# Cross-attention on one core: numerator and denominator from the same PV matmuls, in steps of two heads

## The chip, the core and the metric

The kernel runs on one core of a Trainium2 chip. The metric is the device time of one execution in microseconds (us); lower is better. The engines are PE (matrix multiply), ACT (activation functions), DVE (vector), POOL (GpSimd) and SP, which issues most DMA transfers. Each engine runs its own instructions in order and waits on semaphores for the others.

## The reference

One decoder layer over 64 sequences of 64 tokens, width 256, in float32: layer norm and causal self-attention, then cross-attention without weights, then a layer norm and a mixture of 8 experts (one per token) with a shared expert. The change is in the cross-attention. Its queries are the normalised rows, its keys and values the context rows, and each block is cut into 16 heads of 8 values:

```
qk  = einsum('bdm,bdn->bmn', qh, kh) * scale      # per head: 8 x 256 queries, 8 x 256 keys
sm  = softmax(qk, axis=-1)                        # over the 256 keys n
ret = einsum('bmn,bcn->bcm', sm, vh)              # per head: 8 values of c, 256 columns m
```

So in every head the two indices m and n run over the model's 256 columns, and the 8 values lie along the tokens. A tile is 128 tokens, which is 16 heads. There are NT = 32 tiles. After it, x2 = x1 + ret is normalised, multiplied with the router's weights, and each row is sent to its expert's place in DRAM (xg_d), scaled by the router's sigmoid.

## The kernel before, in words

The program has three stages one after the other: self-attention (`attention`), cross-attention with routing (`cross`), and the experts. This change touches only `cross`, which runs from about 1055 us to 1748 us of the span.

`cross` is a software pipeline over tiles. In the body for tile t, four tiles are in work: t itself (scores for the maximum), w = t-1, v = t-2 and z = t-3. Four bodies at the start and the last ones are written out; tiles 4 to 27 run in a hardware loop of U = 4 bodies, six times round (`tiles`, L849). Within a body every engine steps through 16 heads q, and the `if q == ...` lines of the `body` functions are the only thing that sets the order on each engine.

- `scores_x` (L1139, PE) makes queries by keys of one head in bankX (4 slots), `max_x` (L1052, DVE) reduces two heads at a time to minus the row maximum.
- `split_max` (L929, POOL) splits the 32 columns of maxima in a high and a low part (xhl). It is the first thing POOL does in a body; the last thing of the body before is `send`. `turn_max` (L1179, PE) transposes xhl, `evac_shift` (ACT) copies it, and SP writes it as two extra rows of the queries (L885).
- `turned_scores_x` (L1151, PE), eight heads behind, makes the scores transposed and already shifted in bankXT, which has 2 slots, one head each. It waits until the exponential of the head two before has been taken (`s_xe ... + q - 1`). `exp_x` (L1010, ACT) writes it to one of eight buffers xe.
- `results_x` (L1162, PE) multiplies four heads' exponentials with their values (cT: numerator) and again with a block of ones (onesx: denominator). Four heads use the four 32-column groups of the array at once. It runs four times per tile, at q = 1, 5, 9 and 13.
- `evac_sums` (ACT) copies both to nd, `invert` (DVE) takes the reciprocal of 128x256 denominators in four pieces, and `quotient`, `normalise` and `send` (POOL) divide, add x1, normalise, scale the row and send it with an indirect DMA. `stats_of`, `choose` and `place` (DVE) and `route` (PE) are the statistics and the routing in between.
- SP issues in each body, in this order: the shift rows, the context tile, the loads for tile t+1 (five transfers, 768 KB, L871 and L876), x1, and the stores of xn3 and x2.

Of the kernel before, what the change touches and what calls it, by code (L numbers as in the profile page):

```python
# [760 lines left out]
def cross(nc, A, G, NT, NRT):  # L761
# [6 lines left out]
    with ExitStack() as pb:  # L768
# [3 lines left out]
        def bank(name, n=1):  # L772
# [12 lines left out]
        ones = sb("onesx", [P, 4, 32])  # L785
        onesf = sb("onesf", [P, P])
        half_neg = sb("half_negb", [P, 1])
        spare_g, spare_v = sb("spare_gb", [P, 1]), sb("spare_vb", [P, 1])
# [4 lines left out]
        xe = [sb(f"xe{i}", [P, 2, D]) for i in range(8)]  # L793
        nd = [sb(f"nd{p}", [P, 2, D]) for p in range(2)]
        rden = sb("xrden", [P, D])
        num_ = sb("xnum", [P, D])
# [25 lines left out]
        s_xs, s_xm, s_hl, s_shp, s_shv, s_xst, s_xe, s_xp, s_nd, s_rd, s_num, s_x2 = (  # L822
            sem(n) for n in ("s_xs", "s_xm", "s_hl", "s_shp", "s_shv", "s_xst", "s_xe", "s_xp", "s_nd", "s_rd",
                             "s_num", "s_x2"))
        c_hl, c_ln, g_ln, s_var, s_rstd, s_norm = (
            sem(n) for n in ("c_hl", "c_lnb", "g_lnb", "s_varb", "s_rstdb", "s_normb"))
        s_f3p, s_f3, s_lg, s_top, s_esc, s_oh1, s_rank, s_pos, g_sc, c_fin = (
            sem(n) for n in ("s_f3p", "s_f3", "s_lg", "s_top", "s_esc", "s_oh1", "s_rank", "s_pos", "g_sc", "c_fin"))

        HEADS = [4 * j + (j + b) % 4 for b in range(4) for j in range(4)]  # L830
        LAG = 8
        QUARTER = D // 4
# [16 lines left out]
        def tiles(eng, body):  # L849

            def peeled(t):
                body((t // U, t % U), t < NT, 1 <= t < NT + 1, 2 <= t < NT + 2, 3 <= t)

            for t in range(FIRST):
                peeled(t)
            with eng.Fori(FIRST // U, LAST // U) as h:
                for p in range(U):
                    body((h, p), True, True, True, True)
            for t in range(LAST, NT + 3):
                peeled(t)  # L860
# [4 lines left out]
        def _(sp):  # L865
# [12 lines left out]
            def body(tile, one, two, three, four):  # L878
# [17 lines left out]
                if four:  # L896
                    z = prev(tile, 3)
                    zp = z[1] % 2
                    sp.wait_ge(s_norm, at(z) + 1)
                    sp.dma_start(G.xn3_d[bass.ds(at(z) * P, P), :], xn3[zp][:]).then_inc(s_fst[zp], 16)  # L900
                    sp.dma_start(G.x2_d[bass.ds(at(z) * P, P), :], x2[zp][:]).then_inc(s_fst[zp], 16)

            sp.dma_start(rw[:].rearrange("p k e -> p (k e)"), A["rw"]).then_inc(s_rw, 16)
            load((0, 0))
            sp.dma_start(G.wsh[:], A["wexp"][E]).then_inc(G.s_wsh, 16)
            tiles(sp, body)
# [5 lines left out]
        def _(pool):  # L912
            nc.gpsimd.memset(half_neg[:], -0.5)
            nc.gpsimd.memset(onesf[:], 1.0)
            nc.gpsimd.memset(ones[:], 0.0).then_inc(s_zc, 1)
            pool.wait_ge(s_zc, 1)
            for i in range(4):
                nc.gpsimd.memset(ones[:, i, 8 * i:8 * i + 8], 1.0)
# [3 lines left out]
            pool.wait_ge(s_zc, 2)  # L922

            def settle(tile):

                if inside(tile):
                    nc.gpsimd.tensor_tensor(spare_g[:], half_neg[:], half_neg[:], ALU.mult)

            def split_max(w):  # L929
# [4 lines left out]
                settle(w)  # L934
# [15 lines left out]
            def normalise(z):  # L950
                zp = z[1] % 2
                pool.wait_ge(s_var, at(z) + 1)
                settle(z)
# [3 lines left out]
                need(pool, s_fst[zp], pair(z) * 32)  # L957
                pool.wait_ge(s_rstd, at(z) + 1)
                settle(z)
                nc.gpsimd.tensor_scalar(xn3[zp][:], x2[zp][:], mv[:, 0:1], rstd[:, 0:1], ALU.subtract,  # L960
                                        ALU.mult).then_inc(s_norm, 1)

            def send(z):
                zp = z[1] % 2
                pool.wait_ge(s_esc, at(z) + 1)
                need(pool, s_scat[zp], pair(z) * 16)
                settle(z)
                nc.gpsimd.tensor_scalar(xr[zp][:, 0:D], xn3[zp][:], score[:, 2:3], None, ALU.mult).then_inc(g_sc, 1)
                pool.wait_ge(s_pos, at(z) + 1)
                pool.wait_ge(g_sc, at(z) + 1)  # L970
                nc.gpsimd.indirect_dma_start(
                    out=G.xg_d, out_offset=bass.IndirectOffsetOnAxis(ap=posx[zp][:, 0:1], axis=0),
                    in_=xr[zp][:], in_offset=None,
# [677 lines left out]
```

## Time and profile before

| | us |
|---|---|
| median of 3 runs | 2212.7 (2209.92 to 2214.86) |
| the profiled execution's own time | 2217.57 |
| its span | 2215.7 |
| PE busy | 1992.5 (90%) |
| DVE, ACT, POOL busy | 1181.4, 776.2, 601.4 |

The profile comes from one execution. "Busy" for PE includes the tails of pipelined matmuls, so starts of successive groups are the better measure of what PE does in a time. In the timeline a row is one instruction or several of the same kind merged, with the start, the length, the engine, the line and what it writes and reads; brackets give the idle time before it and who ended it. A float32 matmul that is counted once in the program shows as two records; the scores' matmuls (fp32r) show as one. PEclk is the clock that was granted to PE, as a share of 2.4 GHz.

### The profile page before, as it was taken

How to read it: one execution, taken by the hardware profiler on the slowest of the kernel's cores; microseconds unless marked ns; L12 is line 12 of the kernel's file. 1: busy time of each engine (PE TensorE's matmuls, PEld its weight loads, DVE VectorE, ACT ScalarE, POOL GpSimd, SP SyncE). 2: the span in 40 equal slices, each digit the busy share in tenths (PEclk: the TensorE clock that was granted, in tenths of full speed). 3: DMA queues.
4: the chain of work that ended last, by engine and by line, in shares of the span. 5: the costliest groups of instructions: out<-in, count | busy, mean ns of one | idle time of the engine just before them, and what ended most of it. 6: DMA issues, size and time to landing. Idle time of an engine off the chain costs nothing. (4 is left out here: it accounts for less than half of the span.)

```text
span 2215.7 us, 49383 instructions
## 1 busy us (share of the span) xinstructions
PE 1992.5 (90%) x17585; PEld 1487.9 (67%) x17681; DVE 1181.4 (53%) x2339; ACT 776.2 (35%) x1463; POOL 601.4 (27%) x1094
## 2 busy tenths in 40 slices
PE   4999999999999999994799999999999559999998
PEld 3877778777877778773566666666666336666665
DVE  5566655666566655664766656666665212222222
ACT  3333333333333333331254444544455201111111
POOL 2123222322223222321023323323322210014443
PEclk9999999999999999997799999999999779999999
DMA  5111111111111111111332232232231172222221
GB/s 157 34 40 44 40 47 36 47 36 47 47 36 47 36 47 40 40 42 39 84 79 70 70 79 64 75 80 64 75 79 53 36 269 65 70 65 68 64 66 42
DMA packets 123544, 139.64 MB, mean 63 GB/s; under 512 B 16706, under 2 KB 118086, under 8 KB 121642
## 3 DMA queue, kind: packets, MB, share of 16 engines
q1 hardware_dynamic: 117674, 123.95, 19.7%
q0 software_dynamic: 5760, 14.06, 2.0%
q8 instruction: 89, 1.46, 0.3%
q14 instruction: 21, 0.17, 0.0%
HBM read 85.07 MB, written 53.52 MB: 63 GB/s over the span
## 5 line engine op out<-in xcount | busy, mean ns | idle before, releaser
L1015 ACT ACTIVATE xe<-bankXT 128x512 f32<-128x512 f32 x512 | 289.4, 596 | 326.4 <-PE bankXT L1158 319.4
L1057 DVE TENSOR_REDUCE xmax<-bankX 128x4 f32<-128x1024 f32 x256 | 309.2, 1210 | 135.1 <-PE bankX L1147 135.1
L1147 PE MATMUL bankX<-stk,stq 96*128 96x256 f32 x1024 | 231.6, 312 | 41.7 <-DVE xmax L1057 21.3
L531 DVE TENSOR_TENSOR oTl<-bankV,oTh 128x512 fp32r<-128x512 f32 x128 | 88.5, 691 | 304.5 <-ACT oTh L419 304.5
L1158 PE MATMUL bankXT<-stq,stk 98*128 98x256 f32 x1024 | 222.1, 300 | 8.3 <-ACT xe L1015 4.2
L1147 PEld LDWEIGHTS bankX<-stk,stq 96*128 96x128 f32 x1024 | 163.2, 199 | 72.4 <-issue 47.3
L637 PE MATMUL bankQ<-wqh,xnTh 128*128 128x512 f32 x384 | 188.8, 492 | 0.0
L1158 PEld LDWEIGHTS bankXT<-stq,stk 98*128 98x128 f32 x1024 | 158.8, 193 | 33.7 <-ACT xe L1015 29.2
L1456 DVE TENSOR_TENSOR hid<-bankU,gate 128x512 f32<-128x512 f32 x72 | 49.8, 692 | 244.4 <-PE bankU L1509 237.7
L1402 ACT ACTIVATE gate<-bankG 128x512 f32<-128x512 f32 x72 | 43.0, 597 | 368.9 <-PE bankG L1509 364.2
L350 POOL TENSOR_TENSOR prob<-prob,rden 128x1024 f32<-128x1024 f32 x64 | 121.9, 1904 | 170.6 <-DVE rden L527 170.6
L1173 PE MATMUL bankN<-xe,cT 128*32 128x256 f32 x2048 | 165.2, 395 | 0.2 <-ACT xe L1015 0.2
L1173 PE MATMUL bankN<-xe,onesx 128*32 128x256 f32 x2048 | 162.0, 389 | 0.0
L704 PE MATMUL bankO<-woh,oTh 128*128 128x256 f32 x512 | 155.9, 305 | 6.5 <-DVE oTl L531 3.4
L637 PE MATMUL bankQ<-wql,xnTh 128*128 128x512 f32 x384 | 152.1, 396 | 0.0
L637 PE MATMUL bankQ<-wqh,xnTl 128*128 128x512 f32 x384 | 151.9, 395 | 0.0
L419 ACT ACTIVATE oTh<-bankV 128x512 fp32r<-128x512 f32 x128 | 76.5, 598 | 213.2 <-PE bankV L689 213.2
L614 PE MATMUL bankT<-const,ropeC 128*128 128x128 f32 x640 | 150.1, 275 | 1.0
L614 PE MATMUL bankT<-const,ropeD 128*128 128x128 f32 x640 | 148.4, 273 | 0.0
L318 POOL TENSOR_TENSOR spare_g<-half_neg 128x1 f32<-128x1 f32 x130 | 25.3, 195 | 440.7 <-DVE mv L473 412.5
L704 PE MATMUL bankO<-wol,oTh 128*128 128x256 f32 x512 | 143.4, 280 | 0.0
L704 PE MATMUL bankO<-woh,oTl 128*128 128x256 f32 x512 | 143.0, 279 | 0.0
(173 smaller groups left out, 4053.8 us busy)
## 6 DMA issues: line engine op xcount, KB each, us to landing
stackk_d<-chl SPq DMA_DIRECT2D x96, 128.0 KB, 2.3
stackq_d<-q2hl SPq DMA_DIRECT2D x96, 128.0 KB, 2.3
stk<-stackk_d SPq DMA_DIRECT2D x32, 384.0 KB
stq<-stackq_d SPq DMA_DIRECT2D x128, 96.0 KB
wexp<-in_wexp SPq DMA_DIRECT2D x8, 1536.0 KB, 18.1
x_d<-x SPq DMA_DIRECT2D x64, 128.0 KB, 2.0
xin<-xg_d SPq DMA_DIRECT2D x40, 128.5 KB, 2.0
x<-in_x SPq DMA_DIRECT2D x32, 128.0 KB, 2.2
```

The source lines that it names most:

```text
L350: nc.gpsimd.tensor_tensor(v, v, rden[:, r, :].unsqueeze(2).to_broadcast([P, 16, HD]), ALU.mult).then_inc(s_pn, 1)
L419: nc.scalar.activation(oTh[g % 2][:], bV[:, 0, :].rearrange("p (a b) -> p a b", a=4), ACT.Copy).then_inc(s_oh, 1)
L531: nc.vector.tensor_tensor(oTl[g % 2][:], bV[:, 0, :].rearrange("p (a b) -> p a b", a=4), oTh[g % 2][:].bitcast(F32), ALU.subtract).then_in ...
L614: return nc.tensor.matmul(out, src, ident, is_transpose=True, start=first, stop=final)
L637: ins = nc.tensor.matmul(out, a[p][:, k, :], w[:, k, col:col + 512], start=False, stop=(k == 1 and n == 2))
L704: ins = nc.tensor.matmul(out, a[g % 2][:, j, :], w[:, 4 * g + j, :], start=False, stop=(g == 3 and j == 3 and n == 2))
L1015: nc.scalar.activation(xe[q % 8][:].rearrange("p n m -> p (n m)"), bT[:, q % 2, :], ACT.Exp).then_inc(s_xe, 1)
L1057: nc.vector.tensor_reduce(xmax[tile[1] % 2][:, :, a:b + 1:b - a].rearrange("p m h -> p h m"), bS[:, 2 * (pr % 2):2 * (pr % 2) + 2, :].rear ...
L1147: ins = nc.tensor.matmul(bS[:, q % 4, m * D:(m + 1) * D], stq[p][0:96, hd, m * P:(m + 1) * P], stk[p][0:96, hd // 4, :], start=True, stop= ...
L1158: ins = nc.tensor.matmul(bT[:, q % 2, n * D:(n + 1) * D], stk[p][0:98, hd // 4, n * P:(n + 1) * P], stq[p][0:98, hd, :], start=True, stop= ...
L1173: ins = nc.tensor.matmul(bN[32 * j:32 * j + 32, 0, part * D:(part + 1) * D], lhs, xe[(4 * b + j) % 8][:, k, :], start=(b == 0 and k == 0 a ...
L1456: nc.vector.tensor_tensor(hid[p][:], bS[:, p, :], gate[:], ALU.mult).then_inc(s_h, 1)
```

## The change

- **One PV product.** cT now holds, beside the 8 columns of values of each head, 8 columns of ones, written once at the start. One matmul per head and key half gives 8 rows of numerator and 8 of denominator. The products with onesx are gone, and the two kinds of rows lie interleaved in the two halves of bankN. `results_x` is called twice per tile, with 8 heads each, at steps 1 and 5; xe has 16 buffers.
- **The inverse by DMA.** The denominators of a head are the same in 8 rows. SP gathers one of each (128-byte pieces) to a 128x32 tile `xden`, DVE inverts that (`invert`), SP writes it to DRAM (`inverses_out`) and reads it back 8 times over to `xrden` (`inverses_in`). Where a row holds a denominator, xrden is zero. POOL multiplies all of nd (128x512) with it and adds the two halves to x1 in two operations.
- **Steps of two heads.** A body has 8 steps r; each takes two heads: the turned scores of two heads first, then the scores of two heads. The turned scores of a step wait until the exponentials of both heads of the step before are taken.
- **Other work.** A fifth tile, y = t-4, is in work. `normalise` goes from POOL to DVE, the scaling of the row from POOL to ACT (`scale_row`), the sigmoid's inverse from DVE to POOL (`weigh`). SP's order is new.

The core of the diff:

```diff
-        xe = [sb(f"xe{i}", [P, 2, D]) for i in range(8)]
+        xe = [sb(f"xe{i}", [P, 2, D]) for i in range(XH)]
...
-        LAG = 8
...
+        LAG = 4
+        STEPS = XH // 2
...
+            def inverses_out(z):
+                sp.wait_ge(s_inv, at(z) + 1)
+                for n in range(2):
+                    sp.dma_start(G.inv_d[z[1] % 2, n, :, n, :].rearrange("g (q e) -> g q e", e=32),
+                                 iden[64 * n:64 * n + 64, :]).then_inc(s_invw, 16)
+            def inverses_in(z):
+                sp.wait_ge(s_invw, at(z) * 32 + 32)
+                need(sp, s_num, at(z))
+                for n in range(2):
+                    sp.dma_start(rden[:, n, :], G.inv_d[z[1] % 2, n].rearrange("g s m -> (g s) m").unsqueeze(1)
+                                 .to_broadcast([XH, XD, D])).then_inc(s_rd, 16)
...
+                if four:
+                    inverses_out(z)
+                if five:
+                    yp = y[1] % 2
+                    sp.wait_ge(s_norm, at(y) + 1)
+                    sp.dma_start(G.xn3_d[bass.ds(at(y) * P, P), :], xn3[yp][:]).then_inc(s_fst[yp], 16)
+                    sp.dma_start(G.x2_d[bass.ds(at(y) * P, P), :], x2[yp][:]).then_inc(s_fst[yp], 16)
...
+                if four:
+                    inverses_in(z)
...
+                    vp = v[1] % 2
+                    sp.wait_ge(s_nd, at(v) + 1)
+                    need(sp, s_inv, at(v))
+                    sp.dma_start(den[0:64, :], nd[vp][8::16, 0, :].rearrange("g (q e) -> g q e", e=32)).then_inc(s_den, 16)
+                    sp.dma_start(den[64:128, :], nd[vp][0::16, 1, :].rearrange("g (q e) -> g q e", e=32)).then_inc(s_den, 16)
...
+                    for at_ in (8, 32, 88, 112):
+                        ins = nc.gpsimd.memset(c[:, k, :, at_:at_ + 8], 1.0)
...
             def quotient(z):
                 zp = z[1] % 2
-                pool.wait_ge(s_rd, (at(z) + 1) * 4)
-                nc.gpsimd.tensor_tensor(num_[:], nd[zp][:, 0, :], rden[:], ALU.mult).then_inc(s_num, 1)
+                pool.wait_ge(s_rd, at(z) * 32 + 32)
+                nc.gpsimd.tensor_tensor(part[:], nd[zp][:], rden[:], ALU.mult).then_inc(s_num, 1)
                 pool.wait_ge(s_xa[zp], (pair(z) + 1) * 16)
+                pool.wait_ge(s_num, at(z) + 1)
+                nc.gpsimd.tensor_tensor(whole[:], x1[zp][:], part[:, 0, :], ALU.add).then_inc(s_sum, 1)
                 need(pool, s_fst[zp], pair(z) * 32)
-                pool.wait_ge(s_num, at(z) + 1)
-                nc.gpsimd.tensor_tensor(x2[zp][:], x1[zp][:], num_[:], ALU.add).then_inc(s_x2, 1)
...
+                pool.wait_ge(s_sum, at(z) + 1)
+                nc.gpsimd.tensor_tensor(x2[zp][:], whole[:], part[:, 1, :], ALU.add).then_inc(s_x2, 1)
...
+            def weigh(y):
+                pool.wait_ge(c_fin, at(y) + 1)
+                need(pool, s_xr3, at(y))
+                settle(y, 2)
+                nc.gpsimd.tensor_scalar(score[:, 1:2], score[:, 0:1], 1.0, None, ALU.add).then_inc(g_sc, 1)
+                pool.wait_ge(g_sc, at(y) + 1)
+                nc.gpsimd.tensor_tensor(score[:, 2:3], score[:, 1:2], minus[:], ALU.pow).then_inc(s_esc, 1)
...
+            def body(tile, one, two, three, four, five):
+                z, y = prev(tile, 3), prev(tile, 4)
                 if two:
                     split_max(prev(tile, 1))
+                if five:
+                    weigh(y)
                 if four:
                     quotient(z)
-                    normalise(z)
-                    send(z)
+                    spread(z)
+                if five:
+                    send(y)
...
+            def scale_row(y):
+                yp = y[1] % 2
+                act.wait_ge(s_esc, at(y) + 1)
+                need(act, s_scat[yp], pair(y) * 16)
+                nc.scalar.activation(xr[yp][:, 0:D], xn3[yp][:], ACT.Copy, scale=score[:, 2:3]).then_inc(s_xr3, 1)
-                if q % 4 == 0:
-                    need(act, s_xp, at(w) * 4 + q // 4 - 1)
-                nc.scalar.activation(xe[q % 8][:].rearrange("p n m -> p (n m)"), bT[:, q % 2, :],
+                if q % 8 == 0:
+                    need(act, s_xp, at(w) * 2 + q // 8 - 1)
+                nc.scalar.activation(xe[q][:].rearrange("p n m -> p (n m)"), bT[:, q % 2, :],
...
+            def body(tile, one, two, three, four, five):
+                w, v, z, y = prev(tile, 1), prev(tile, 2), prev(tile, 3), prev(tile, 4)
+                for r in range(STEPS):
+                    if two and r == 1:
                         evac_shift(w)
+                    if five and r == 2:
+                        act.wait_ge(s_f3p, at(y) + 1)
                         nc.scalar.activation(xn3T[:], bM[:, 0, 0:D].rearrange("p (k n) -> p k n", k=2),
                                              ACT.Copy).then_inc(s_f3, 1)
+                    if five and r == 4:
+                        act.wait_ge(s_top, at(y) + 1)
+                        nc.scalar.activation(score[:, 0:1], top8[:, 0:1], ACT.Exp, scale=-1.0).then_inc(c_fin, 1)
+                    if five and r == 6:
+                        scale_row(y)
+                    if three and r == 6:
                         evac_sums(v)
+                    if two and r == 7:
+                        evac_ctx(w)
+                    if two and r >= LAG:
+                        exp_x(w, 2 * (r - LAG))
+                        exp_x(w, 2 * (r - LAG) + 1)
+                    if three and r < LAG:
+                        exp_x(v, 2 * (r + STEPS - LAG))
+                        exp_x(v, 2 * (r + STEPS - LAG) + 1)
...
+            def invert(z):
+                dve.wait_ge(s_den, at(z) * 32 + 32)
+                need(dve, s_invw, at(z) * 32)
+                nc.vector.reciprocal(iden[:], den[:]).then_inc(s_inv, 1)
...
+            def body(tile, one, two, three, four, five):
+                z, y = prev(tile, 3), prev(tile, 4)
+                routing = Chain(dve, c_rt, 4, at(y))
+                for r in range(STEPS):
+                    if one:
+                        max_x(tile, r)
+                    if four and r == 0:
+                        invert(z)
+                    if five and r == 0:
+                        normalise(y)
+                    if five and r == 3:
+                        choose(y, routing)
+                    if five and r == 5:
+                        place(y, routing)
+                    if four and r == 6:
                         stats_of(z)
...
+            def turned_scores_x(w, r):
                 h, p = w
-                if q == 0:
+                if r == 0:
                     pe.wait_ge(s_sh[p], (h + 1) * 32)
-                need(pe, s_xe, at(w) * XH + q - 1)
...
+                need(pe, s_xe, at(w) * XH + 2 * r)
+                for q in (2 * r, 2 * r + 1):
+                    hd = HEADS[q]
+                    for n in range(2):
+                        ins = nc.tensor.matmul(bT[:, q % 2, n * D:(n + 1) * D],
+                                               stk[p][0:98, hd // 4, n * P:(n + 1) * P],
+                                               stq[p][0:98, hd, :], start=True, stop=True)
+                    ins.then_inc(s_xst, 1)
...
+            def results_x(v, g):
+                c = cT[v[1] % 2][:].rearrange("p k h c -> p k (h c)")
+                pe.wait_ge(s_xe, at(v) * XH + 8 * g + 8)
+                if g == 0:
+                    pe.wait_ge(s_cT, at(v) + 1)
+                    need(pe, s_nd, at(v))
+                for b in (2 * g, 2 * g + 1):
+                    for k in range(2):
                         for j in range(4):
+                            m = (j + b) % 4
+                            ins = nc.tensor.matmul(bN[32 * j:32 * j + 32, 0, (m % 2) * D:(m % 2 + 1) * D],
+                                                   c[:, k, 160 * j + 32 * m:160 * j + 32 * m + 32],
+                                                   xe[4 * b + j][:, k, :],
+                                                   start=(b == 0 and k == 0), stop=(b >= 2 and k == 1),
                                                    skip_group_check=True)
...
+            def body(tile, one, two, three, four, five):
+                w, v, y = prev(tile, 1), prev(tile, 2), prev(tile, 4)
+                for r in range(STEPS):
+                    if two and r >= LAG:
+                        turned_scores_x(w, r - LAG)
+                    if three and r < LAG:
+                        turned_scores_x(v, r + STEPS - LAG)
                     if one:
+                        scores_x(tile, r)
+                    if three and r == 1:
+                        results_x(v, 0)
+                    if three and r == 5:
+                        results_x(v, 1)
+                    if two and r == 0:
                         turn_max(w)
+                    if five and r == 1:
+                        turn_norm(y, two)
+                    if five and r == 2:
+                        logits(y)
+                    if five and r == 4:
+                        rank(y)
+                    if two and r == 6:
                         turn_ctx(w)```

On PE, in the loop body before, from the second head's turned scores to the transposed maxima (bankX: scores, bankXT: turned scores, bankN: numerator and denominator, bankM: small transposes, xhl: the split maxima):

```order
L1158 MATMUL bankXT<-stq,stk 128x256 x2
L1173 MATMUL bankN<-xe,cT 32x256 x4
L1173 MATMUL bankN<-xe,onesx 32x256 x4
L1173 MATMUL bankN<-xe,cT 32x256 x4
L1173 MATMUL bankN<-xe,onesx 32x256 x4
L1147 MATMUL bankX<-stk,stq 128x256 x2
L103 REGISTER_ALU
L1158 MATMUL bankXT<-stq,stk 128x256 x2
L1180 REGISTER_ALU
L103 REGISTER_ALU
L1130 MATMUL bankM<-const,xhl 32x128 x2
```

The same place now, the first rows of a body, on PE:

```order
L1201 MATMUL bankXT<-stq,stk 128x256 x4
L1184 ISA
L103 ISA
L1189 MATMUL bankX<-stk,stq 128x256 x4
L1225 REGISTER_ALU
L103 REGISTER_ALU
L1179 MATMUL bankM<-const,xhl 32x128 x2
L103 REGISTER_ALU
L1201 MATMUL bankXT<-stq,stk 128x256 x4
L1189 MATMUL bankX<-stk,stq 128x256 x4
L1217 MATMUL bankN<-xe,cT 32x256 x16
```

The transposed maxima stood behind three heads and a PV block of the body; now they stand behind two heads, at the end of step 0, and the PV run comes after them in step 1.

On POOL, at the border between two bodies before (L960 normalises, L968 scales the row, L971 sends it, L935 and L937 split the maxima):

```order
L960 TENSOR_SCALAR xn_1<-x_1,mvb,rstdb 128x256
L103 REGISTER_ALU
L927 TENSOR_TENSOR spare_gb<-half_negb 128x1
L968 TENSOR_SCALAR xr<-xn_1,score 128x256
L971 REGISTER_ALU
L971 DMA xg_d<-xr,posx 33792x257
L932 ISA
L927 TENSOR_TENSOR spare_gb<-half_negb 128x1
L935 CAST xhl<-xmax 128x2x16
L937 TENSOR_TENSOR xhl<-xmax,xhl 128x2x16
```

And now (L980 adds the second half to x, L986 and L988 are `spread`, L1003 sends, L965 and L967 split):

```order
L980 TENSOR_TENSOR x_1<-xwhole,xpart 128x256
L957 TENSOR_TENSOR spare_gb<-half_negb 128x1
L986 TENSOR_SCALAR rstdb<-mvb 128x1
L988 TENSOR_TENSOR rstdb<-rstdb,half_negb 128x1
L1003 REGISTER_ALU
L1003 DMA xg_d<-xr,posx 33792x257
L962 ISA
L957 TENSOR_TENSOR spare_gb<-half_negb 128x1
L965 CAST xhl<-xmax 128x2x16
L967 TENSOR_TENSOR xhl<-xmax,xhl 128x2x16
```

Normalising and scaling are gone from POOL; the send now stands behind `spread`, which waits for DVE's statistics at step 6 (`stats_of`, which came at head 3 before).

## Rows read from the trace of the kernel before

**Rows 1.** Windows: busy us of each engine (instructions), PEclk, DMA share, GB/s

```profile
1350.00:1370.00 20.00, 18.81 (x209) 13.48 (x207) 13.38 (x31) 10.29 (x22) 6.68 (x13) 1.00 0.28 76
```

**Rows 2.** Groups by line, 1260 to 1660 us: busy us, mean ns | idle before

```profile
L1015 ACT ACTIVATE xe<-bankXT 128x512 f32<-128x512 f32 x312 | 176.6, 596 | 204.2 <-PE bankXT L1158 200.3
...
L1173 PE MATMUL bankN<-xe,cT 128*32 128x256 f32 x1240 | 100.5, 397 | 0.0
L1173 PE MATMUL bankN<-xe,onesx 128*32 128x256 f32 x1236 | 98.0, 389 | 0.0
...
L1037 ACT ACTIVATE score<-top 128x1 f32<-128x1 f32 x20 | 3.9, 195 | 0.0
```

**Rows 3.** Timeline of PE in one body: start, length

```profile
1500.59 0.39 PE L1130 MATMUL bankM<-const,xhl 128*32 128x128 f32 x2 [1.25 <-POOL xhl L937]
...
1502.15 0.50 PE L1158 MATMUL bankXT<-stq,stk 98*128 98x256 f32 x2
1502.58 0.64 PE L1173 MATMUL bankN<-xe,cT 128*32 128x256 f32 x8
...
1504.45 0.44 PE L1130 MATMUL bankM<-const,cx 128*128 128x128 f32 x2
...
1505.20 0.40 PE L1147 MATMUL bankX<-stk,stq 96*128 96x256 f32 x2
1505.43 0.40 PE L1158 MATMUL bankXT<-stq,stk 98*128 98x256 f32 x2
...
1520.36 0.39 PE L1130 MATMUL bankM<-const,xhl 128*32 128x128 f32 x2 [1.16 <-POOL xhl L937]
```

**Rows 4.** The tile of split maxima, all 32 tiles: ns min/median/max, first and last start

```profile
L935 POOL CAST xhl<-xmax x32: 210/213/223, 1074.6 to 1701.6; 128x32 fp32r<-128x32 f32 x32
```

**Rows 5.** Timeline around a back edge of the loop, and the last back edge

```profile
1205.13 0.50 PE L1147 MATMUL bankX<-stk,stq 96*128 96x256 f32 x2 [2.38 <-DVE xmax L1057]
...
1206.38 1.08 PE L1173 MATMUL bankN<-xe,cT 128*32 128x256 f32 x8
...
1209.76 0.50 PE L1147 MATMUL bankX<-stk,stq 96*128 96x256 f32 x2
...
1537.73 0.79 PE L1147 MATMUL bankX<-stk,stq 96*128 96x256 f32 x2 [2.49 <-DVE xmax L1057]
```

**Rows 6.** Timeline in the drain of the stage, PE and ACT, without new scores

```profile
1716.79 0.71 PE L1158 MATMUL bankXT<-stq,stk 98*128 98x256 f32 x4
...
1717.31 2.28 ACT L1015 ACTIVATE xe<-bankXT 128x512 f32<-128x512 f32 x4 [2.05 <-PE bankXT L1158]
1717.96 0.99 PE L1158 MATMUL bankXT<-stq,stk 98*128 98x256 f32 x4 [0.45 <-ACT xe L1015]
...
1725.26 1.08 ACT L1015 ACTIVATE xe<-bankXT 128x512 f32<-128x512 f32 x2 [1.70 <-PE bankXT L1158]
```

**Rows 7.** Timeline of DVE and POOL in the body of rows 3

```profile
1502.40 0.42 DVE L1073 BATCH_NORM_STATS2 statsb<-x 128x6 f32<-128x256 f32 x1
...
1503.61 0.57 POOL L956 TENSOR_TENSOR rstdb<-rstdb,half_negb 128x1 f32<-128x1 f32 x1
...
1505.63 1.23 DVE L1057 TENSOR_REDUCE xmax<-bankX 128x4 f32<-128x1024 f32 x1 [1.46 <-PE bankX L1147]
...
1518.44 1.15 POOL L971 DMA_INDIRECT xg_d<-xr,posx  x1 [0.89 <-POOL xr L968]
1519.62 0.20 POOL L927 TENSOR_TENSOR spare_gb<-half_negb 128x1 f32<-128x1 f32 x1
```

**Rows 8.** Windows behind the stall of rows 5, and in the drain

```profile
1206.00:1210.00 4.00, 4.00 (x37) 1.77 (x37) 1.23 (x1) 1.08 (x2) 2.98 (x6) 0.57 0.09 33
1704.00:1706.00 2.00, 2.00 (x25) 1.03 (x28) 0.36 (x2) 0.68 (x2) 1.24 (x3) 0.61 0.07 16
```

**Rows 9.** DMA issues from 1300 to 1600 us: KB each, median us to landing

```profile
xn_d<-xn SPq DMA_DIRECT2D x15, 128.0 KB, 3.6
...
stq<-sh SPq DMA_DIRECT2D x28, 16.0 KB, 2.2
```

More of the change, by code:

```diff
@@ L857, in tiles @@
                 for p in range(U):
-                    body((h, p), True, True, True, True)
-            for t in range(LAST, NT + 3):
+                    body((h, p), True, True, True, True, True)
+            for t in range(LAST, NT + 4):
                 peeled(t)
@@ L913, in _ @@
             nc.gpsimd.memset(half_neg[:], -0.5)
+            nc.gpsimd.memset(minus[:], -1.0)
             nc.gpsimd.memset(onesf[:], 1.0)
[L915 to L918, printed above, removed]
             for p in range(2):
@@ L976, in body, with send @@
-            def body(tile, one, two, three, four):
-                z = prev(tile, 3)
+            def weigh(y):
[5 more added lines that the diff above has]
+                nc.gpsimd.tensor_tensor(score[:, 2:3], score[:, 1:2], minus[:], ALU.pow).then_inc(s_esc, 1)
+            def send(y):
+                yp = y[1] % 2
+                pool.wait_ge(s_pos, at(y) + 1)
+                pool.wait_ge(s_xr3, at(y) + 1)
+                nc.gpsimd.indirect_dma_start(
+                    out=G.xg_d, out_offset=bass.IndirectOffsetOnAxis(ap=posx[yp][:, 0:1], axis=0),
+                    in_=xr[yp][:], in_offset=None,
+                    bounds_check=at(y) + G.XROWS).then_inc(s_scat[yp], 16)
@@ L1052, in max_x @@
             def max_x(tile, pr):
[L1053 removed]
+                dve.wait_ge(s_xs, at(tile) * STEPS + pr + 1)
                 if pr == 0:
@@ L1206, in body, with turn_norm @@
-            def body(tile, one, two, three, four):
-                w, v, z = prev(tile, 1), prev(tile, 2), prev(tile, 3)
-                for q in range(XH):
-                    if one:
-                        scores_x(tile, q)
-                    if two and q >= LAG:
-                        turned_scores_x(w, q - LAG)
-                    if three and q < LAG:
-                        turned_scores_x(v, q + XH - LAG)
-                    if two and q == LAG + 5:
-                        results_x(w, 0)
-                    if three and q in (LAG - 7, LAG - 3, LAG + 1):
-                        results_x(v, (q - LAG + 11) // 4)
-                    if two and q == 2:
-                        turn_max(w)
-                    if two and q == 5:
+            def turn_norm(y, two):
+                pe.wait_ge(s_norm, at(y) + 1)
+                pe.wait_ge(s_shv, at(y) + 4 if two else NT)
+                for i in range(2):
+                    ins = turn(bM[:, 0, i * P:(i + 1) * P], xn3[y[1] % 2][:, i * P:(i + 1) * P])
+                ins.then_inc(s_f3p, 1)
@@ new lines, in turn_ctx, with body @@
+            def turn_ctx(w):
+                pe.wait_ge(s_cx[w[1] % 2], (pair(w) + 1) * 16)
+                pe.wait_ge(s_shv, at(w) + 1)
+                need(pe, s_pos, at(w) - 2)
+                for k in range(2):
+                    ins = turn(bM[:, 0, k * P:(k + 1) * P], ctx[w[1] % 2][:, k * P:(k + 1) * P])
+                ins.then_inc(s_cTp, 1)
+            def body(tile, one, two, three, four, five):
+                w, v, y = prev(tile, 1), prev(tile, 2), prev(tile, 4)
[4 more added lines that the diff above has]
+                        turned_scores_x(v, r + STEPS - LAG)
+                    if one:
+                        scores_x(tile, r)
[4 more added lines that the diff above has]
+                    if two and r == 0:
+                        turn_max(w)
+                    if five and r == 1:
[5 more added lines that the diff above has]
+                    if two and r == 6:
@@ L1222, in body @@
                         turn_ctx(w)
-                    if four:
-                        route(z, q, two)
             tiles(pe, body)
```

192 lines of the change are left out of this document (56 added, 136 removed).

## The prediction

> **What bounds the kernel now.** I read four views. First the windows of the cross-attention stage: in 20 us PE is busy for 18.81, DVE for 13.38, ACT for 10.29, and the granted clock is 1.00, that is 2.4 GHz [rows 1]. PE bounds this stage, and nothing else is near. Second, the groups by line: the PV products with cT and those with onesx cost PE nearly the same, 100.5 and 98.0 us in 400 [rows 2]. Third, the timeline of one body. Two matmuls of one head's scores start 0.24 us before the next two, a PV block (cT, ones, cT, ones) takes 1504.45 - 1502.58 = 1.87 us, and its entry costs 0.43 - 0.24 = 0.19 more, so a block is 2.06 us [rows 3]. Fourth, the pace: the split maxima come 32 times between 1074.6 and 1701.6 us, 20.23 us per tile [rows 4]. Part of it is the loop's back edge: from the first to the last of five, PE resumes at 1205.13 and 1537.73 us, 83.15 us for four tiles, where an undisturbed body takes 19.77 (1500.59 to 1520.36 [rows 3]), 79.08 for four. A back edge so costs 4.1 us, five of them 20, and the other pace is (627 - 20) / 31 = 19.6 us.
>
> Two more things bear on the change. An undisturbed body already holds one PE stall, 1.16 or 1.25 us until POOL has split the maxima [rows 3]. And the clock falls behind long stalls: after the 2.38 us at a back edge the clock is 0.57 [rows 8], and a PV block takes 1209.76 - 1206.38 = 3.38 us instead of 1.87 [rows 5].
>
> **What the change removes.** Per tile four PV blocks become two runs. A run has 16 matmuls with 32 columns, as many as a block had, so 1.87 + 0.19 = 2.06 us each. PE loses 4.12 us per tile. On PE alone a tile would be about 15.5 us. But then something else is late, in two places, and I add up a body step by step.
>
> **The ping-pong with ACT.** bankXT has two slots. Before, PE filled one while ACT emptied the other. Now PE waits until both are empty. From the drain: turned scores start at 1716.79, the first exponential at 1717.31 (0.52 later), and PE goes on at 1717.96, 0.05 after that exponential's 0.60 [rows 2] is over; two exponentials take 1.08 [rows 6]. A plain step is 0.52 + 1.08 + 0.05 = 1.65, with a little for the semaphores 1.67 us. PE's own work in it is 8 matmuls, 4 x 0.24 = 0.96, so it waits 0.7 us in every such step.
>
> The steps, from the start of a step's turned scores to the next:
> - Step 1: 0.96 + 2.06 (PV) + 0.14 (transposes of xn3), 3.16, bound by PE.
> - Steps 2, 3 and 7: 1.67 each, 5.01. The logits in step 2 lie in the wait.
> - Step 4: ACT first takes the exponential of the top logit, for which DVE must have finished the maximum of step 3 and one short operation. DVE starts that maximum 0.72 + 0.43 us into step 3 (second head's scores, then 1505.63 - 1505.20 [rows 3, 7]), it takes 1.23 [rows 7], the short one as long as ACT's by estimate, 0.20 each [rows 2]: the exponentials start 2.7 us after step 3 began instead of 1.67 + 0.52 = 2.2. 1.67 + 0.5 = 2.17.
> - Step 5: 0.96 + 2.06, 3.02. Step 6: 1.67 and 0.1 for the sums' copy, 1.77.
>
> **The POOL chain at the border.** In step 0, after 0.96 us of work, PE wants the split maxima. POOL can only split when it has sent tile y, and it sends only after `spread`, which waits for DVE's statistics in step 6. In time from the start of step 6: DVE starts its maximum at 0.72 + 0.43 = 1.15 and ends at 2.38; from the statistics' start to the end of the power on POOL it is 1503.61 + 0.57 - 1502.40 = 1.78, so 4.16; the send takes 1.15, and before it stand 0.89 us of idle time [rows 7]. Whether these 0.89 come again I can't see: before, the send waited for its own row's scaling; now nothing new is waited for. From 0 to 0.89, and I take half. So 5.31 to 6.20, then 0.03 and from POOL's next operation to PE 1520.36 - 1519.62 = 0.74 [rows 3, 7]. PE gets its maxima at 6.08 to 6.97. Steps 6 and 7 last 3.44, so this is 2.6 to 3.5 us into step 0; with the transposes' 0.15 step 0 takes about 3.2 instead of 1.67.
>
> The sum is 3.2 + 3.16 + 5.01 + 2.17 + 3.02 + 1.77 = 18.3 us per tile (17.9 to 18.8), against 19.6.
>
> **The other edits.** DVE loses four reciprocals and gets one of 128x32 and the normalising; it has 8 x 1.23 us of maxima in 18 and stays clear. ACT gets the row's scaling, in step 6, where it waits for the PV run anyway. The inverse's way through three pairs of small transfers is off the path while it has slack: denominators are gathered after step 6's copy and needed 1.5 us behind their landing in step 0, taking 2.2 us for a landing [rows 9]; inverses are back some 9.5 us into the body and POOL wants them at 12; the shift rows, now queued behind three waits of SP, land about 1.6 us before step 4 uses them. The next tile's loads, issued about 8 to 10 us into the body, have 6 us left. So these cost nothing, as long as a landing stays under about 4 us.
>
> The back edge before costs 4.1 us: 2.4 of PE's stall and the rest of slow clock. Now a body starts with waits for ACT and POOL, and most of the stall falls into them: I take 1.0 each, 5 instead of 20. The drain gets a stage more, with three landings in its chain, but its bodies are shorter: +2.
>
> Without the clock: 31 x (18.3 - 19.6) = -40, -15 for the back edges, +2: -53 us.
>
> **The clock.** At the border PE will now idle from 0.96 to 3.05 us of step 0, 2.1 us, after a step in which it idled 0.7. Before, the stall of 1.2 us inside busy work left the clock at 1.00 [rows 1, 3], the 2.38 us one of a back edge did [rows 8], and so did the other four. 2.1 us with 0.7 close by is nearer to the second. The slow stretch then falls on step 1, which is PE's: up to 3.38 - 1.87 = 1.5 us [rows 5], less where it lies over waits. I take 1.3 for 30 tiles, +39. The bounds are 0 (never falls) and, with falls in other steps too, 2.5.
>
> The Trainium skill speaks against that term: "TensorE: Matmul & The Clock Gate", section "Why this matters for your kernels", warns only of idle gaps longer than any in this stage. By it the clock would never fall, and the forecast would be rival A. The rows of this case disagree with the page already at 2.38 us.
>
> Forecast: 2217.57 - 53 + 39 = 2203.6 us for a profiled execution; that one ran 4.9 above the median, so about 2198.
>
> **The rivals.**
> - A: the clock stays up. For it: stalls of 1.2 us in each body leave it at 1.00 [rows 1, 3], and no stall here is as long as the 2.38 us of a back edge. Against: 2.1 us is nearer to that than to 1.2. 2212.7 - 53 = 2160; with the 0.89 us hidden 0.45 x 31 = 14 less, 2146.
> - C, slower: the clock falls in the ping-pong steps too. They leave PE idle for 0.7 of 1.67 us, and in the drain the clock was 0.61 right behind waits that were each under 1 us [rows 8]. Then the run in step 5 is hit as well: 1.3 + 0.7 + about 0.5 in the plain steps, 2.5 per tile, 31 x 2.5 = 78: 2212.7 - 53 + 78 = 2238. It decides from 1.7 us per tile (53 / 31) upward.
> - D: the transfers are late. A landing of 3.6 us, as the 128 KB stores show [rows 9], on each of the three small ones eats the slack of 1.5 to 2.4 us; 1 us per tile beyond it costs 31: 2229. Against: the queue is nearly empty in that part of the body.
>
> **How the numbers follow.** Forecast 0.40 (its own range 2180 to 2214), A 0.27, C 0.23, D 0.10. The range takes in A without its hidden part's end and C: 2150 to 2238. Differences within 0.2% (4.4 us) can't be told from none. Faster: A and most of the forecast's share, 0.61; same 0.10; slower 0.29.
>
> **What would show it.** Right: about 2.06 us per PV run and two runs per tile; exponentials in pairs with PE waiting for them in each plain step; a wait of PE for POOL's xhl of 1 to 2 us per tile; the granted clock of the stage between 0.85 and 0.95; bodies 19 to 20.3 us apart. Clock 1.00 means A, under 0.8 C. Waits for DMA on stq, xden or xrden mean D. It is wrong in its root if PE does not wait for ACT in the plain steps, or POOL has split the maxima before PE comes.

## The result and the profile after

The changed kernel takes 2235.57 us median (2230.65 to 2238.2), before 2212.49 in the same comparison: 1.0105 times as long, 95% interval 1.0093 to 1.0118. I had forecast 2198 and faster, with a range of 2180 to 2214; only the slower rival C (2238) came near. The span of the profiled execution is 2235.4 us. All ratios here are to the kernel before, run again in the same comparison. It took 2212.5 to 2217.5 us there, so differences in us between runs of different comparisons are good to some 5 us.

Page of the kernel after, the sums and the slices:

```profile
PE 1949.3 (87%) x15632; PEld 1467.7 (66%) x15633; DVE 1149.1 (51%) x2211; ACT 792.3 (35%) x1495; POOL 596.1 (27%) x1114
...
PEclk9999999999999999996788889888888679999999
```

PE has 43 us less to do by its busy time, and the digits of PEclk over the cross-attention fell from 9 to 8. The windows (columns as in [rows 1]) of the stage's middle, and the pace (as in [rows 4]):

```profile
1260.00:1660.00 400.00, 332.73 (x2675) 244.05 (x2676) 227.70 (x482) 199.04 (x413) 121.88 (x242) 0.84 0.31 83
```

```profile
L965 POOL CAST xhl<-xmax x32: 210/218/224, 1073.8 to 1713.4; 128x32 fp32r<-128x32 f32 x32
```

The granted clock is 0.84. As it has two levels, 1.2 and 2.4 GHz, PE ran slow for 0.32 of the time, 128 us in these 400, or 6.7 us for each of the 19 tiles in them. Tiles come every (1713.4 - 1073.8) / 31 = 20.63 us on average, against 20.23. This average takes in three short ones at the start (13.9, 16.2 and 16.5 us); from then on it is 21.2.

One body in the timeline of PE (as [rows 3]); it begins at 1504.18 with step 0:

```profile
1501.80 0.38 PE L1179 MATMUL bankM<-const,cx 128*128 128x128 f32 x2
1502.51 0.75 PE L1201 MATMUL bankXT<-stq,stk 98*128 98x256 f32 x4 [0.32 <-ACT xe L1057]
1503.09 0.64 PE L1189 MATMUL bankX<-stk,stq 96*128 96x256 f32 x4
1504.18 0.74 PE L1201 MATMUL bankXT<-stq,stk 98*128 98x256 f32 x4 [0.46 <-ACT xe L1057]
1504.76 0.64 PE L1189 MATMUL bankX<-stk,stq 96*128 96x256 f32 x4
1507.14 0.39 PE L1179 MATMUL bankM<-const,xhl 128*32 128x128 f32 x2 [1.74 <-POOL xhl L967]
1507.29 0.72 PE L1201 MATMUL bankXT<-stq,stk 98*128 98x256 f32 x4
...
1508.42 1.93 PE L1217 MATMUL bankN<-xe,cT 128*32 128x256 f32 x32
...
1512.17 0.74 PE L1201 MATMUL bankXT<-stq,stk 98*128 98x256 f32 x4 [0.16 <-ACT xe L1057]
...
1513.85 0.74 PE L1201 MATMUL bankXT<-stq,stk 98*128 98x256 f32 x4 [0.46 <-ACT xe L1057]
...
1516.08 1.11 PE L1201 MATMUL bankXT<-stq,stk 98*128 98x256 f32 x4
...
1517.97 2.74 PE L1217 MATMUL bankN<-xe,cT 128*32 128x256 f32 x32
1520.64 0.74 PE L1201 MATMUL bankXT<-stq,stk 98*128 98x256 f32 x4
```

The reader sees the ping-pong (plain steps 1.67 us apart, a bracket for ACT in each), the maxima 2.96 us into step 0, and the first PV run at full clock in 1.9 us but the second in 2.7: the matmuls of step 5 are slow from its start on (1.11 us for four where 0.74 is usual), so the clock fell in step 4. In the body before it was the other run that was slow:

```profile
1485.84 0.61 PE L1179 MATMUL bankM<-const,xhl 128*32 128x128 f32 x2 [1.73 <-POOL xhl L967]
1486.10 1.20 PE L1201 MATMUL bankXT<-stq,stk 98*128 98x256 f32 x4
1487.10 1.05 PE L1189 MATMUL bankX<-stk,stq 96*128 96x256 f32 x4
1488.09 3.64 PE L1217 MATMUL bankN<-xe,cT 128*32 128x256 f32 x32
```

POOL at the same border shows the chain, with 0.24 us before the send where it had been 0.89 [rows 7]:

```profile
1504.42 0.57 POOL L988 TENSOR_TENSOR rstdb<-rstdb,half_negb 128x1 f32<-128x1 f32 x1
1505.24 1.13 POOL L1003 DMA_INDIRECT xg_d<-xr,posx  x1 [0.24 <-issue]
1506.40 0.21 POOL L957 TENSOR_TENSOR spare_gb<-half_negb 128x1 f32<-128x1 f32 x1
```

### The profile page after: what moved, and what is told of

The parts are those of the page before. It is cut to its first block and busy times, and to the rows that moved or that the text cites. A ratio compares the mean times of both kernels' runs of the same rounds, so it can differ in the third digit from the quotient of the medians.

```text
span 2235.4 us, 45480 instructions
## 1 busy us (share of the span) xinstructions
PE 1949.3 (87%) x15632; PEld 1467.7 (66%) x15633; DVE 1149.1 (51%) x2211; ACT 792.3 (35%) x1495; POOL 596.1 (27%) x1114
## 5 line engine op out<-in xcount | busy, mean ns | idle before, releaser
L1057 ACT ACTIVATE xe<-bankXT 128x512 f32<-128x512 f32 x512 | 277.0, 593 | 82.8 <-PE bankXT L1201 81.7
L1201 PE MATMUL bankXT<-stq,stk 98*128 98x256 f32 x1024 | 206.4, 328 | 47.5 <-ACT xe L1057 44.4
L1189 PE MATMUL bankX<-stk,stq 96*128 96x256 f32 x1024 | 186.2, 311 | 30.2 <-DMA stq<-stackq_d 20.7
L1201 PEld LDWEIGHTS bankXT<-stq,stk 98*128 98x128 f32 x1024 | 153.2, 209 | 90.0 <-ACT xe L1057 66.2
L1189 PEld LDWEIGHTS bankX<-stk,stq 96*128 96x128 f32 x1024 | 161.2, 217 | 32.5 <-issue 21.5
L1217 PE MATMUL bankN<-xe,cT 128*32 128x256 f32 x2048 | 178.6, 509 | 0.4 <-ACT xe L1057 0.4
L689 PE MATMUL bankV<-probT,vbd 128*128 128x256 f32 x512 | 135.4, 387 | 6.0 <-ACT probT L413 4.9
## 6 DMA issues: line engine op xcount, KB each, us to landing
stackk_d<-chl SPq DMA_DIRECT2D x96, 128.0 KB, 2.3
stackq_d<-q2hl SPq DMA_DIRECT2D x96, 128.0 KB, 2.3
x_d<-x SPq DMA_DIRECT2D x64, 128.0 KB, 1.8
xrden<-inv_d SPq DMA_DIRECT2D x64, 128.0 KB, 2.5
```

The lines of the kernel that those rows point to most:

```text
L689: ins = nc.tensor.matmul(out[:, :, b, :], vbd[u[1]][b][:, g, :], src[:, :, b, :], start=True, stop=True)
L1057: nc.scalar.activation(xe[q][:].rearrange("p n m -> p (n m)"), bT[:, q % 2, :], ACT.Exp).then_inc(s_xe, 1)
L1189: ins = nc.tensor.matmul(bS[:, q % 4, m * D:(m + 1) * D], stq[p][0:96, hd, m * P:(m + 1) * P], stk[p][0:96, hd // 4, :], start=True, stop= ...
L1201: ins = nc.tensor.matmul(bT[:, q % 2, n * D:(n + 1) * D], stk[p][0:98, hd // 4, n * P:(n + 1) * P], stq[p][0:98, hd, :], start=True, stop= ...
L1217: ins = nc.tensor.matmul(bN[32 * j:32 * j + 32, 0, (m % 2) * D:(m % 2 + 1) * D], c[:, k, 160 * j + 32 * m:160 * j + 32 * m + 32], xe[4 * b ...
```

## Experiments

My theory after the result: the waits in the plain steps and the one at the border (PE's wait for xhl in step 0) cost their own length, as worked out; what was too small is the slow clock they bring. The rivals: only the border's wait matters (B), only the plain steps' (P), or the clock is a by-product.

**The send before `spread`**, so that the split is no longer behind it:

```diff
                 if four:
                     quotient(z)
-                    spread(z)
                 if five:
                     send(y)
+                if four:
+                    spread(z)
```

> The changed kernel with one edit: POOL sends tile y before spread(z), not behind it, so that the split of the maxima no longer waits for the indirect DMA. PE should want the maxima 1.0 us into step 0 and get them at about 1.6 instead of 2.96: 1.3 us per tile of waiting gone, 31 x 1.3 = 40 us. Theory B (the wait at the border is what lowers the clock): the slow stretches go as well, mean clock of the stage from 0.84 to above 0.95, 2155 to 2170 us. Theory P (the 0.7 us waits in the plain steps lower it just as much): clock stays near 0.85, about 2195 us. Rival S (the split is bound by DVE's last maximum, not by the send): no change, 2235 us.

2130.38 us, 0.9627 of before (0.9611 to 0.9643). That is 105 us under the changed kernel, more than either number expected. The border:

```profile
1500.07 0.74 PE L1202 MATMUL bankXT<-stq,stk 98*128 98x256 f32 x4 [0.46 <-ACT xe L1058]
1500.65 0.63 PE L1190 MATMUL bankX<-stk,stq 96*128 96x256 f32 x4
1501.69 0.40 PE L1180 MATMUL bankM<-const,xhl 128*32 128x128 f32 x2 [0.40 <-POOL xhl L967]
1501.84 0.72 PE L1202 MATMUL bankXT<-stq,stk 98*128 98x256 f32 x4
```

The maxima come 1.62 us into step 0 instead of 2.96, the next ones at 1518.70, 17.01 us on. The waits of the plain steps are unchanged (0.46). This kernel's stage ends earlier, so its clock is read from 1160 to 1560 us: 0.99, against 0.84 in the changed kernel over the same window.

```profile
L965 POOL CAST xhl<-xmax x32: 208/209/215, 1074.5 to 1603.9; 128x32 fp32r<-128x32 f32 x32
```

From the first to the last split the stage is (1713.4 - 1073.8) - (1603.9 - 1074.5) = 110 us shorter. PE's waits for xhl in the whole stage sum to 13.7 us where they were 51.5, 38 us less. I put the other 72 down to slow clock: the other waits of PE are as long as before, and only one is new, of 1.5 us. (The whole program gains 105; what comes behind the last split is longer by the rest.)

**Useless matmuls where PE waits.** The scores are issued `again` times over before their semaphore, five times in step 0 and twice in steps 2, 3, 4, 6 and 7. Two more runs have only the first part of this, or only the second:

```diff
-                for q in (2 * r, 2 * r + 1):
+                again = {0: 5, 2: 2, 3: 2, 4: 2, 6: 2, 7: 2}.get(r, 1)
+                for q in [2 * r] * again + [2 * r + 1] * again:
```

> The changed kernel with useless work on PE: the scores' matmuls into bankX are repeated before their semaphore, 5 times in step 0, twice in steps 2, 3, 4, 6 and 7, so that PE works where it waited (36 x 0.12 = 4.3 us more matmul time per tile at full clock), with the same results. If the slow clock costs what I think (2 us per tile), the clock rises to above 0.95 and the kernel gets faster by 40 to 60 us, 2175 to 2195, in spite of the work. If the clock is only a by-product and the waits are the whole cost, it is the same or slower, 2235 to 2280.

> As the fill in all steps, but in step 0 alone (16 more matmuls, 1.9 us, where PE waits for the split maxima). Theory B (the border causes the slow stretches): nearly the whole gain of the fill in all steps, 2180 to 2200, clock above 0.93. Theory P (the plain steps cause them): little, 2225 to 2240, clock under 0.88.

> As the fill in all steps, but only in the plain steps 2, 3, 4, 6 and 7 (20 more matmuls, 0.48 us in each wait of 0.7). Theory P: most of the gain, 2180 to 2205. Theory B: the border's stall of 1.9 us still lowers the clock once per tile in front of the PV run of step 1, 2220 to 2240, clock under 0.90.

| fill | us | ratio to before (95%) | clock, 1260 to 1660 us |
|---|---|---|---|
| all | 2194.68 | 0.992 (0.9904 to 0.9937) | 1.00 |
| step 0 only | 2215.87 | 1.0015 (1.0005 to 1.0025) | 0.91 |
| plain steps only | 2244.78 | 1.0146 (1.013 to 1.0163) | 0.90 |

With 36 more matmuls per tile the kernel is 41 us faster than without, so the clock is a cause. Neither half does it alone. For the border filled, B expected at most 2200 us and P at least 2225; for the plain steps filled, B at most 2240 and P at most 2205. Neither theory fits both rows, though B comes closer in the second. One body in the timeline of PE with all filled, from the turned scores of step 4 on:

```profile
1503.25 0.74 PE L1202 MATMUL bankXT<-stq,stk 98*128 98x256 f32 x4
...
1505.41 0.39 PE L1248 MATMUL bankM<-onehot,const 128*128 128x8 f32 x2 [0.46 <-DVE onehot L1139]
...
1505.96 0.74 PE L1202 MATMUL bankXT<-stq,stk 98*128 98x256 f32 x4
...
1512.41 0.74 PE L1202 MATMUL bankXT<-stq,stk 98*128 98x256 f32 x4
...
1516.06 0.72 PE L1202 MATMUL bankXT<-stq,stk 98*128 98x256 f32 x4
```

The fill has a price of its own, since the last scores reach DVE later: step 4 takes 2.71 us (2.23 in the body of the changed kernel above) and step 0 3.65 (3.11), together 1.0 us per tile, 32 us. With the 41 us gained, the clock had cost some 73, about what the send first gave.

With the border filled the clock falls behind the plain steps, where a late shift transfer adds to their waits. From 1160 to 1560 us PE waits for it 18 times, 15.4 us in all, which the changed kernel does not do; so this run does not test B alone:

```profile
1512.83 1.20 PE L1202 MATMUL bankXT<-stq,stk 98*128 98x256 f32 x4 [0.70 <-DMA stq<-sh]
...
1517.37 3.06 PE L1218 MATMUL bankN<-xe,cT 128*32 128x256 f32 x32
```

With the steps filled it falls behind the border (2.33 us of waiting there instead of some 1.8, as the chain starts later). No run kept the border as it was and only shortened the plain steps' waits, so their share stays open.

**A useless POOL operation** between `spread` and the split, in the kernel with the send first, once and twice:

```diff
                     spread(z)
+                    nc.gpsimd.tensor_tensor(idle_b[:, 0:256], idle_a[:, 0:256], idle_a[:, 0:256], ALU.mult)
```

> The changed kernel with the send before spread (2130 us), and a useless 128x256 operation on POOL (about 0.73 us) between spread and the split of the maxima. It puts back half of the wait at the border, with no DMA in it: from 0.4 to about 1.1 us. As a mere wait 31 x 0.73 = 23 us, 2153. If a wait of this length already lowers the clock: up to 2190.

> The same with two such operations (about 1.45 us): the wait at the border is then 1.8 us, as in the changed kernel, whose send had put it there. As a mere wait 31 x 1.45 = 45 us, 2175. If the length of this wait is what lowers the clock, as I think, then all of the lost time comes back: 2220 to 2240, clock of the stage about 0.84.

The groups of the border's matmuls from 1160 to 1560 us (two records a tile), with the send first, then with one and with two such operations:

```profile
L1180 PE MATMUL bankM<-const,xhl 128*32 128x128 f32 x46 | 9.0, 278 | 9.6 <-POOL xhl L967 9.6
```

```profile
L1183 PE MATMUL bankM<-const,xhl 128*32 128x128 f32 x40 | 8.3, 292 | 19.4 <-POOL xhl L969 19.4
```

```profile
L1184 PE MATMUL bankM<-const,xhl 128*32 128x128 f32 x38 | 9.2, 332 | 28.6 <-POOL xhl L969 28.6
```

With a border wait of 0.42 (9.6 / 23), 0.97 and 1.51 us on average the kernel takes 2130.38, 2203.57 and 2236.25 us (ratios 0.9627, 0.9935 with 0.9919 to 0.9952, and 1.0083 with 1.0067 to 1.01). The first operation costs more than the 2190 us that I had named as its upper end. Waiting 0.55 us longer costs 68 us by the ratios (73 by the times), 2.2 per tile; 1.1 us longer costs 101 to 106, nearly the whole loss, with no DMA in the wait. The clock from 1160 to 1560 us is 0.99, 0.88 and 0.84. This is the shortest proof: the wait costs three to four times its own length.

It does not decide body by body. With one operation there are two kinds of body behind nearly the same wait:

```profile
1403.43 0.40 PE L1183 MATMUL bankM<-const,xhl 128*32 128x128 f32 x2 [0.89 <-POOL xhl L969]
...
1420.92 0.39 PE L1183 MATMUL bankM<-const,xhl 128*32 128x128 f32 x2 [0.89 <-POOL xhl L969]
...
1441.61 0.39 PE L1183 MATMUL bankM<-const,xhl 128*32 128x128 f32 x2 [0.95 <-POOL xhl L969]
...
1462.19 0.49 PE L1183 MATMUL bankM<-const,xhl 128*32 128x128 f32 x2 [0.87 <-POOL xhl L969]
```

From the first to the second row it is 17.49 us, at clock 1.00: this is the 17.0 of the send first with 0.49 more of waiting, so this body pays the wait's length and nothing else. From the third to the fourth it is 20.58, at clock 0.83, so this one pays 3.1 us of slow clock on top. Of the 20 bodies from 1166.94 to 1560.44 us, 7 are of the first kind and 13 take 20.5 us or more. What puts a body in one kind or the other stays open.

**Head by head**: scores then turned scores of one head, with the wait of the kernel before; once with the changed kernel's POOL order, and once with the send first. The line of the edit that sets the wait:

```diff
-                need(pe, s_xe, at(w) * XH + 2 * r)
+                need(pe, s_xe, at(w) * XH + q - 1)
```

> The changed kernel with one edit: PE goes head by head again (scores of a head, then turned scores of a head, each waiting only for the exponential two heads before), so both slots of bankXT are in use; POOL's order stays as in the changed kernel. My theory (the wait for the split maxima at the border, with the slow clock behind it, is the cause): steps 2, 3, 4, 5, 6 and 7 shrink by up to 0.4 us each, but the time from step 6 to the split maxima is fixed, so what steps 6 and 7 gain is waited for in step 0; 0.4 x 3 = 1.2 us per tile at best, 2195 to 2235 us, and the clock no higher than 0.86. Rival (the ping-pong with ACT is the cause): 2.4 us per tile or more, under 2160.

> Head by head as above, and the send before spread as in the run that gave 2130. With the border's wait short, the steps' gain counts: ping-pong 0.46 us in steps 2 to 7 gone or halved, 0.8 to 1.5 us per tile, 2085 to 2110 us, clock 0.97 or more. If ACT or DVE bound the steps anyway: 2125 to 2135.

2204.11 us (ratio 0.9947, 0.9931 to 0.9964) and 2109.32 (0.9517, 0.9501 to 0.9533). The first is as expected: what the steps save is partly waited for at the border, 2.47 us, and the clock is 0.83:

```profile
1504.10 0.61 PE L1179 MATMUL bankM<-const,xhl 128*32 128x128 f32 x2 [2.47 <-POOL xhl L967]
```

So the ping-pong is worth 21 to 31 us, the border with its clock 95 to 105. The second has the time that I expected, but not the clock: 0.93 from 1160 to 1560 us where I had said 0.97 or more. PE waits there 1.1 us for xhl and 0.7 us for the onehot in each body.

**The PV products twice**, in the kernel with the send first:

```diff
-                        for j in range(4):
+                        for again in range(2):
+                            for j in range(4):
```

> The changed kernel with the send before spread, and every PV matmul issued twice (numerator and denominator double alike, so the quotient stays): the PE work of the products with ones is back, the new order stays. It measures what the halving of the PV products is worth where nothing else is late: 2 x 1.74 us per tile, 31 tiles, 108 us, so 2130 + 108 = 2238 us at a clock near 1.00, if the PV steps are bound by PE throughout. If ACT's or POOL's chains hide part of it, less: down to 2200.

2236.06 us (1.0084, 1.0062 to 1.0106), at clock 1.00: the halving of the PV work is worth 106 us (101 by the ratios) once nothing else is late. A doubled run takes 3.66 us instead of 1.93, and two of them in 31 tiles are 107.

**The kernel before with its send behind the split**, one tile later:

```diff
                     split_max(prev(tile, 1))
+                if five:
+                    send(prev(tile, 4))
                 if four:
                     quotient(z)
                     normalise(z)
-                    send(z)
```

> The kernel before, with POOL's send moved behind the split of the maxima of the next body (one tile later): takes away its own wait of 1.2 us for the split maxima, with the old PV products. If that wait is worth its length there, 31 x 1.1 = 34 us less, 2175 to 2185; if the gain of the edited changed kernel (105 us) came from the send alone and not from the PV products, this kernel would come near 2130 too.

A miss: 2233.44 us (1.008, 1.006 to 1.0099). The wait for xhl goes, 18.1 us in the kernel before from 1260 to 1660 us. In its place PE waits longer for DVE's maxima (16.5 us, where it was 9.6) and, now new, for the rows that POOL normalises (12.2 us). Both fit with quotient and statistics coming later; that chain was not traced further:

```profile
1515.51 0.50 PE L1157 MATMUL bankX<-stk,stq 96*128 96x256 f32 x2 [0.66 <-DVE xmax L1067]
...
1517.14 0.43 PE L1140 MATMUL bankM<-const,xn 128*128 128x128 f32 x2 [0.90 <-POOL xn L960]
```

It still shows that moving POOL's send is no gain by itself in the old order.

**Two further orders**, in the kernel head by head with the send first. In the one, ACT takes the exponential of the top logit behind step 4's own:

```diff
-                    if five and r == 4:
-                        act.wait_ge(s_top, at(y) + 1)
...
                         exp_x(v, 2 * (r + STEPS - LAG) + 1)
+                    if five and r == 4:
+                        act.wait_ge(s_top, at(y) + 1)
```

> Head by head and send first, and on ACT the exponential of the top logit behind the two exponentials of step 4 instead of before them. It waited for DVE's choice with two exponentials behind it (0.5 us per tile): 10 to 15 us under the same kernel without this edit, if PE waits for those exponentials there; nothing if PE waits for DVE's onehot in step 4 anyway.

2110.82 us (0.9518, 0.9499 to 0.9537): no difference from 2109.32; PE waits for the onehot there anyway. In the other, PE turns the split maxima in step 1 and makes the rank sums in step 5, each one step later, and ACT empties the shift rows behind step 1's exponentials. On PE:

```diff
+                    if two and r == 1:
+                        turn_max(w)
+                    if five and r == 5:
+                        rank(y)
                     if three and r == 1:
                         results_x(v, 0)
...
-                    if two and r == 0:
-                        turn_max(w)
...
-                    if five and r == 4:
-                        rank(y)
```

> Head by head and send first (2109 us), and on PE the transposes of the split maxima moved behind the scores of step 1 and the routing's rank matmuls behind the scores of step 5, with the copy of the shift behind the exponentials of step 1 on ACT. The waits of 1.07 us for xhl and 0.71 us for the onehot, per tile, should go: up to 31 x 1.7 = 53 us, 2060 to 2085. Rival: the shift rows come 1 us later and turned scores at step 4 wait for their DMA instead, 2100 to 2120.

2069.32 us (2068.47 to 2075.56), 0.9339 of before (0.932 to 0.9358): the best version, 6.6% under the kernel before, at clock 0.98. The waits for xhl and the onehot are gone. What is left are mostly transfers: from 1160 to 1560 us PE waits for the shift rows, as the rival said, 22 times and 8.9 us in all, and for the next tile's loads 16 times, 8.5 us.

## Why the prediction was wrong, point by point

- **PV.** Right: two runs of 1.93 us by the row, at full clock, and 101 to 106 us for their halving.
- **Ping-pong.** Right: 1.67 us a step (1512.17 to 1513.85 is 1.68). Step 4 measured 2.23 against 2.17.
- **POOL chain.** Right: 2.96 us into step 0, against 2.6 to 3.5.
- **The body as a whole.** Right: with the send first and the clock at 0.99 it is 17.01 us, and with the 1.34 us of waiting that this order saves it is 18.35, against the sum of 18.3.
- **The back edges.** I took 1.0 us each, from no row. With the send first, PE's wait for xhl is 0.55 instead of 0.40 in every fourth body and the body 17.16 us instead of 17.01, so I read 0.15 for a back edge. The profile's queue of instruction transfers (q8) has 37 in the changed kernel, 38 with the send first and 89 before. That this is why the stall of 2.4 us went was not tested.
- **Transfers (rival D).** Not the cause: in the whole stage PE waits for a transfer once, 20.7 us for the first loads, as before the change (20.4).
- **The drain.** I took +2. From the last xhl to the next stage's first ACT instruction it was 1751.33 - 1701.6 = 49.7 us and is 1769.72 - 1713.4 = 56.3, +6.6. With the fill it is 57.1 and with the send first 58.0, so it does not hang on the border's wait. Which part of the drain was sized wrong was not traced.
- **The clock: the step that failed**, as I put it: "I take 1.3 for 30 tiles, +39." I priced one slow stretch per tile, on step 1 alone. The stage ran slow for 6.7 us per tile, and in one of the two bodies shown it was step 5 that paid. My own sum without the clock gives a pace of 18.3 + 5/31 = 18.5, so the clock costs 20.63 - 18.5 = 2.1 us per tile, 66 us instead of 39. Two runs say about the same without that sum: 72 us with the send first, 73 with the fill. The PV runs alone show most of it, in the groups from 1260 to 1660 us (columns as in [rows 2]), 106.8 us for 19 tiles, 5.6 each, where two runs at full clock are 3.9:

```profile
L1217 PE MATMUL bankN<-xe,cT 128*32 128x256 f32 x1216 | 106.8, 512 | 0.0
```

With +66 and +6.6 in their places the sum gives 2212.7 - 53 + 66 + 5 = 2231, near the 2235.57 measured. That it closes is no proof, since the 66 is the measured pace less the sum; the two runs are. I looked for a length of stall above which the clock falls, found 1.2 us harmless and 2.4 not, and put 2.1 once between them. But the 1.2 us were harmless in the old body, where PE hardly waited elsewhere; in a body with steps in which PE idles 0.46 us, a wait of 0.87 to 1.21 us came with slow clock in 13 bodies of 20. Rival C had that mechanism, with 0.23, though its sign, a clock under 0.80, was not met (0.84).

The page of the Trainium skill that I weighed, "TensorE: Matmul & The Clock Gate", section "Why this matters for your kernels", was no guide here: the gaps that its warning names are longer than any in these bodies, and the clock was at 0.84 all the same.

## What to carry to other kernels

When a change thins out the engine that was full, price the clock over the whole body: look at all the waits that stand near each other, not only at the longest one. An operation at the end of one tile's queue that stands in front of the next tile's first one (here an indirect DMA on POOL) is the first thing to move; one moved call was worth 105 us here. And test a stall by filling it with useless work: if that is faster, the clock is a cause. Last, read a wait as an average over many bodies before you put a price on it.

## What the runs showed of the hardware

- PE with 36 useless matmuls more per tile ran the program 41 us faster, at clock 1.00 instead of 0.84.
- The same kernel with one wait of 0.42, 0.97 and 1.51 us per tile on average: 2130, 2204 and 2236 us, at clock 0.99, 0.88 and 0.84.
- With the same wait of 0.9 us, bodies of one kernel took 17.5 us at clock 1.00 or 20.6 us at clock 0.83.
- The idle time before the indirect DMA was 0.89 us behind an operation on the row it sends, and 0.24 where the instruction before was unrelated; no run varied this alone.
